# Scores and the product with V' as four column tiles of 32 rows in place of two of 64, in a cross-attention and feed-forward kernel

## The chip, the cores and the metric

One core of one Trainium2 chip. The metric is device microseconds of one execution. The engines are TensorE (PE in the profile, PEld for its weight loads), VectorE (DVE), ScalarE (ACT), GpSimd (POOL) and SyncE (SP), each with its own instruction stream; they meet through semaphores.

## What is computed

128 sequences of 64 tokens of 128 features (`x`) attend to 128 context sequences of the same shape, and a feed-forward part follows:

```python
def xattn(q, k, v, Wq, Wk, Wv, Wo, bo, mask):      # 16 heads of 64
    qh = split_heads(q @ Wq)
    kh = split_heads(k @ Wk)
    vh = split_heads(v @ Wv)
    dots = einsum('bhid,bhjd->bhij', qh, kh) * 64 ** -0.5
    dots = where(mask or causal, -max, dots)
    out = einsum('bhij,bhjd->bhid', softmax(dots), vh)
    return merge_heads(out) @ Wo + bo
x = x + xattn(layernorm(x), ctx, ctx, ...)
x = x + bitlinear(silu(bitlinear(layernorm(x), w_gate)) * bitlinear(layernorm(x), w_up), w_down)
```

`bitlinear` rounds its input to 8 bits by row and its weights to -1, 0, 1 times a scale.

## The kernel before, in words

The 8,192 tokens are taken as 64 pairs of sequences, 128 tokens each; four pairs are a group that is loaded with one DMA. The projections are folded: M = Wk Wq^T and N = Wv Wo are made once for each head in the setup, so that with K' = M ctx and V' = ctx N the scores of a head are x_norm K' and its output is prob V', both with 128 features in the middle or at the end. M, N and the context are each split in a high and a low part (`F32R`), and K' and V' are three matmuls each (`k_unit`, lines 323 to 325; `v_quarter`, lines 403 to 405).

Every engine runs the same list of slots, one a pair: eight written out, then a hardware loop over eight slots that is run six times (`slots`, whose loop is line 202), then eight written out and three of tail. In a slot TensorE does, in this order, which is written out by hand:

- the scores of pair s (line 432): for each half of the heads (8 heads x 64 keys are 512 columns, one bank of `ps_s`) and each of the two sequences b, one float32 matmul call whose stationary operand is that sequence's 64 columns of `xn_t` and whose output is 64 of the 128 partitions. Sequence b = 0 writes partitions 0 to 63 and b = 1 writes 64 to 127, so the two use different column tiles of the array. In the profile a float32 call is two weight loads and two matmuls.
- the transpose of the quantised rows of pair s - 1 (line 445, it waits for VectorE's `xq_b`, line 839), four of the hidden rows of pair s - 3 (line 453), the transposes of the probabilities of pair s - 1 (line 460), gate and up (lines 473, 474), the down product (line 489), among them the quarters of V' of pair s and of K' of the next group
- the product with V' of pair s - 1 (line 501): for each of 8 pairs of heads `a` and each sequence b one float32 call, stationary 64 columns of `prob_t`, moving 128 columns of `vp`, accumulated over `a` in `ps_a[b * S:(b + 1) * S, 0:D]`. It waits for `pt_evac`, `v_evac` and `x2_done` (the wait before it is line 498).
- two quarters of K' and V' more (the wait value of the last V' quarters is made at line 399), and after every fourth slot eight transposes of the next but one group (lines 281 and 317).

ScalarE evacuates K', V' and the transposes (line 521) and does the exponential (line 577). VectorE adds the bias to the scores (line 745, which signals `biased`), takes maxima and sums (lines 748, 821), adds the residual to the product with V' (line 808) and does the layer norms and the quantisation; once a group it makes the low part of the context (line 679). GpSimd subtracts the maxima and multiplies by the reciprocals (lines 875, 893). The setup's M products (line 310) have 64 rows: heads of one parity stand in rows 0 to 63 and write `ps_s`, those of the other stand in rows 64 to 127 and write `ps_kv`, in this order of the program, 16 matmuls each.

Of the kernel before, what the change touches and what calls it, by code (L numbers as in the profile page):

```python
# [32 lines left out]
P = 128  # L33
# [7 lines left out]
def build(nc, x, ctx, mask, wq, wk, wv, wo, bo, w_gate, w_up, w_down, ident, causal, chooser, out):  # L41
    B, S, D = x.shape
# [3 lines left out]
    HP = H // 2  # L46
# [7 lines left out]
    BANK = 512  # L54
# [6 lines left out]
    with ExitStack() as es:  # L61
# [5 lines left out]
        ps_s = ps("ps_s", 2)  # L67
        ps_kv = ps("ps_kv", 2)
        ps_a = ps("ps_a", 1)
# [29 lines left out]
        xn_t = [sb(f"xn_t{i}", [P, GP * P]) for i in range(2)]  # L99
# [5 lines left out]
        vp = [sb(f"vp{i}", [P, 2, HP, D]) for i in range(2)]  # L105
        prob = [sb(f"prob{i}", [P, H, S]) for i in range(2)]
        prob_t = sb("prob_t", [P, HP, P])
# [75 lines left out]
        def live(it, c, back=0):  # L183

            return not isinstance(it, int) or 0 <= BODY * it + c - back < PAIRS

        def group_ahead(it, c, n):

            return not isinstance(it, int) or 2 * it + c // GP + n < GROUPS

        def first(it, c):
            return isinstance(it, int) and it == 0 and c == 0
# [74 lines left out]
        def _(pe):  # L267
            mm = nc.tensor.matmul
# [5 lines left out]
            for k in range(8):  # L274
                mm(banks[k], choose[:], mask_bf[:, k * BANK:(k + 1) * BANK],
                   start=True, stop=True).then_inc(maskrow_ready, 1)
# [28 lines left out]
            for par in range(2):  # L305
                r = slice(DH * par, DH * par + DH)
                for half in range(2):
                    for k in range(4):
                        a = 4 * half + k
                        t = mm(banks[2 * par + half][:, k * P:(k + 1) * P], w_t[0][r, a, :], w_t[1][r, a, :],  # L310
                               start=True, stop=True)
# [72 lines left out]
            def slot(it, c):  # L384
                s = BODY * it + c
                g, q, par = 2 * it + c // GP, c % GP, c // GP % 2
# [31 lines left out]
                if live(it, c):  # L418

                    if q == 0:  # L420
                        pe.wait_ge(k_evac, 16 * g + 16)
                        pe.wait_ge(xnt_evac, g + 1)
                    if first(it, c):
                        pe.wait_ge(mean_done, 1)
                    if live(it, c, 1):
                        pe.wait_ge(v_evac, 8 * s - 2)
                        if not isinstance(it, int) or group_ahead(it, c - 1, 1):
                            pe.wait_ge(k_evac, 16 + 4 * s - 1)
                    for half in range(2):
                        for b in range(2):  # L430
                            cols = slice(q * P + b * S, q * P + b * S + S)
                            t = mm(ps_s[b * S:(b + 1) * S, half * BANK:(half + 1) * BANK], xn_t[par][:, cols],  # L432
                                   kp[par][:, half * 8:half * 8 + 8, cols], start=True, stop=True)
                    t.then_inc(scores_ready, 1)
                if first(it, c):
# [13 lines left out]
                if live(it, c, 3):  # L449

                    pe.wait_ge(hb_ready, s - 2)
                    for k in range(FB):
                        t = nc.tensor.transpose(ps_h[:, k * P:(k + 1) * P], hid_b[:, k * P:(k + 1) * P], id_bf[:])
# [29 lines left out]
                if live(it, c, 3):  # L483
# [4 lines left out]
                    for k in range(FB):  # L488
                        t = mm(ps_a[:, D:2 * D], hid_t[:, k, :], wd_t[:, k, :], start=(k == 0), stop=(k == FB - 1))
# [3 lines left out]
                if live(it, c, 1):  # L493

                    pe.wait_ge(pt_evac, 2 * s)
                    pe.wait_ge(v_evac, 8 * s)
                    if live(it, c, 3):
                        pe.wait_ge(x2_done, s - 2)
                    for a in range(HP):
                        for b in range(2):  # L500
                            t = mm(ps_a[b * S:(b + 1) * S, 0:D], prob_t[:, a, b * S:(b + 1) * S],  # L501
                                   vp[(c - 1) % 2][:, b, a, :], start=(a == 0), stop=(a == HP - 1))
                    t.then_inc(attn_ready, 1)
                v_quarter(2)
                k_quarter(2)
# [2 lines left out]
                if live(it, c) and q == GP - 1 and group_ahead(it, c, 2):  # L508
# [5 lines left out]
                    transpose_x(par)  # L514

            slots(pe, slot, 4 - 1)


# [405 lines left out]
```

## Time and profile before

| | |
|---|---|
| median of 3 runs | 829.24 us (828.57 to 829.48) |
| the profiled execution, first to last instruction (its span) | 827.9 us |
| mean granted TensorE clock of it | 0.991 |
| TensorE matmuls, busy | 781.9 us (94%) |
| VectorE, busy | 738.6 us (89%) |
| ScalarE, busy | 679.7 us (82%) |
| GpSimd, busy | 407.3 us (49%) |

The profile gives no time of that execution other than its span; the medians contain what lies around it. Matmuls overlap, and their ends are modelled by the profiler, so rates are taken from starts. In the rows L501 is line 501; `128*64 128x512` is 128 rows and 64 columns of stationary operand and a moving operand of 128 rows and 512 columns. Groups of the same kind that follow each other are merged, with their count behind an x; such a row's duration is from the first start to the last end, less idle time.

### The profile page before, as it was taken

How to read it: one execution, taken by the hardware profiler on the slowest of the kernel's cores; microseconds unless marked ns; L12 is line 12 of the kernel's file. 1: busy time of each engine (PE TensorE's matmuls, PEld its weight loads, DVE VectorE, ACT ScalarE, POOL GpSimd, SP SyncE). 2: the span in 40 equal slices, each digit the busy share in tenths (PEclk: the TensorE clock that was granted, in tenths of full speed). 3: DMA queues.
4: the chain of work that ended last, by engine and by line, in shares of the span. 5: the costliest groups of instructions: out<-in, count | busy, mean ns of one | idle time of the engine just before them, and what ended most of it. 6: DMA issues, size and time to landing. Idle time of an engine off the chain costs nothing.

```text
span 827.9 us, 17931 instructions
## 1 busy us (share of the span) xinstructions
PE 781.9 (94%) x5487; PEld 539.4 (65%) x5550; DVE 738.6 (89%) x1909; ACT 679.7 (82%) x1202; POOL 407.3 (49%) x404
## 2 busy tenths in 40 slices
PE   7899999999999999999999999999999999999873
PEld 5657666766766666676666667567666666766552
DVE  6759999999989998999989999899989999988994
ACT  4689888888888888888888898888888888888772
POOL 1235555454544644545455554455554555545551
PEclk9999999999999999999999999999999999999996
DMA  7200010100101010010100101010010100000000
GB/s 214 62 1 1 15 39 15 39 1 15 39 14 38 13 35 4 13 38 13 38 4 21 28 13 38 14 38 0 13 39 13 38 13 13 2 13 14 1 14 13
DMA packets 37108, 20.49 MB, mean 25 GB/s; under 512 B 1460, under 2 KB 36534, under 8 KB 37046
## 3 DMA queue, kind: packets, MB, share of 16 engines
q1 hardware_dynamic: 37046, 19.84, 8.3%
q14 instruction: 45, 0.37, 0.2%
q8 instruction: 17, 0.28, 0.1%
HBM read 15.64 MB, written 4.19 MB: 24 GB/s over the span
## 4 chain that ended last, share of the span: by engine, by line
PE 52%; DVE 31%; issue 11%; ACT 3%; DVEq 1%; POOL 1%; DMA 0%; POOLq 0%; ACTq 0%
PE ps_a L501 9%; PE ps_s L432 7%; DVE row_sum L821 5%; DVE xq_b L839 3%; PE ps_s L403 3%; DVE amax L778 2%; DVE hid L775 2%; PE ps_s L323 2%; PE ps_a L460 2%; PE ps_b L460 2%; PE ps_kv L403 2%; PE ps_s L325 2%; PE ps_kv L323 2%; PE ps_s L404 2%; PE ps_s L324 2%
## 5 line engine op out<-in xcount | busy, mean ns | idle before, releaser
L875 POOL TENSOR_TENSOR prob<-prob,row_max 128x1024 f32<-128x1024 f32 x64 | 122.0, 1906 | 194.1 <-DVE row_max L748 194.1
L521 ACT ACTIVATE vp<-ps_s 64x512 f32<-64x512 f32 x256 | 151.4, 591 | 32.8 <-PE ps_s L405 28.5
L893 POOL TENSOR_TENSOR prob<-prob,row_rec 128x512 f32<-128x512 f32 x128 | 130.9, 1044 | 56.2 <-DVE row_rec L823 56.2
L521 ACT ACTIVATE vp<-ps_kv 64x512 f32<-64x512 f32 x256 | 151.6, 592 | 5.4
L885 POOL TENSOR_TENSOR hid_b<-hid_q,neg_round 128x512 bf16<-128x512 f32 x64 | 66.6, 1041 | 130.1 <-DVE hid_q L792 130.1
L432 PE MATMUL ps_s<-kp,xn_t 128*64 128x512 f32 x512 | 124.0, 605 | 2.9 <-ACT vp L521 1.9
L501 PE MATMUL ps_a<-vp,prob_t 128*64 128x128 f32 x2048 | 125.9, 276 | 0.8 <-DVE x L770 0.6
L501 PEld LDWEIGHTS ps_a<-vp,prob_t 128*64 128x64 f32 x2048 | 110.6, 137 | 24.0 <-issue 16.4
L852 POOL TENSOR_TENSOR rs<-ve,neg_half 128x1 f32<-128x1 f32 x128 | 70.4, 550 | 35.5 <-DVE ve L670 25.4
L745 DVE TENSOR_TENSOR prob<-ps_s,bias_sb 128x1024 f32<-128x1024 f32 x64 | 78.2, 1222 | 10.7 <-PE ps_s L432 9.9
L521 ACT ACTIVATE kp<-ps_s 128x512 f32<-128x512 f32 x130 | 77.8, 598 | 12.0 <-PE ps_s L291 8.2
L748 DVE TENSOR_REDUCE row_max<-prob 128x16 f32<-128x1024 f32 x64 | 78.1, 1220 | 2.2
L821 DVE TENSOR_REDUCE row_sum<-prob 128x16 f32<-128x1024 f32 x64 | 77.4, 1210 | 0.0
L521 ACT ACTIVATE xq_t<-ps_u 128x128 bf16<-128x128 bf16 x64 | 17.8, 278 | 68.0 <-PE ps_u L445 68.0
L521 ACT ACTIVATE kp<-ps_kv 128x512 f32<-128x512 f32 x122 | 72.3, 592 | 0.6 <-PE ps_kv L291 0.5
L432 PEld LDWEIGHTS ps_s<-kp,xn_t 128*64 128x64 f32 x512 | 31.0, 136 | 60.5 <-issue 46.5
L577 ACT ACTIVATE prob<-prob 128x1024 f32<-128x1024 f32 x64 | 66.9, 1045 | 0.0
L839 DVE TENSOR_SCALAR xq_b<-xq 128x128 bf16<-128x128 f32 x64 | 61.2, 956 | 2.2
L403 PE MATMUL ps_s<-n_hi,ct_hi 128*128 128x512 f32 x128 | 62.4, 487 | 0.7 <-ACT vp L521 0.7
L403 PE MATMUL ps_kv<-n_hi,ct_hi 128*128 128x512 f32 x128 | 61.3, 479 | 0.0
L323 PE MATMUL ps_kv<-ct_hi,m_hi 128*128 128x512 f32 x120 | 52.6, 438 | 1.0 <-ACT wd_t L521 1.0
L323 PE MATMUL ps_s<-ct_hi,m_hi 128*128 128x512 f32 x128 | 52.1, 407 | 0.4
(176 smaller groups left out, 1767.6 us busy)
## 6 DMA issues: line engine op xcount, KB each, us to landing
x_in<-in_x SPq DMA_DIRECT2D x16, 256.0 KB, 3.0
ctx_in<-in_ctx SPq DMA_DIRECT2D x16, 256.0 KB, 3.4
x_res<-in_x SPq DMA_DIRECT2D x16, 256.0 KB, 2.8
out<-x SPq DMA_DIRECT2D x15, 256.0 KB, 2.3
kp<-in_L_xattn_Wk SPq DMA_DIRECT2D x1, 512.0 KB, 4.5
kp<-in_L_xattn_Wq SPq DMA_DIRECT2D x1, 512.0 KB, 5.3
kp<-in_L_xattn_Wv SPq DMA_DIRECT2D x1, 512.0 KB, 6.2
kp<-in_L_xattn_Wo SPq DMA_DIRECT2D x1, 512.0 KB, 6.1
```

Of the source, the lines that this page charges most:

```text
L323: mm(dst, hi, ct_hi[par][:], start=True, stop=False)
L403: mm(v_dst, ct_hi[par][:, cols], hi, start=True, stop=False)
L432: t = mm(ps_s[b * S:(b + 1) * S, half * BANK:(half + 1) * BANK], xn_t[par][:, cols], kp[par][:, half * 8:half * 8 + 8, cols], start=True, ...
L501: t = mm(ps_a[b * S:(b + 1) * S, 0:D], prob_t[:, a, b * S:(b + 1) * S], vp[(c - 1) % 2][:, b, a, :], start=(a == 0), stop=(a == HP - 1))
L521: copy = lambda dst, src, **kw: nc.scalar.activation(dst, src, ACT.Copy, **kw)
L745: v.tensor_tensor(prob[c % 2][:], ps_s[:, :].rearrange("p (h j) -> p h j", j=S), pair_bias.broadcast_to([P, H, S]), ALU.add).then_inc(bias ...
L748: v.tensor_reduce(row_max[c % 2][:], prob[c % 2][:], AX, ALU.max).then_inc(max_done, 1)
L821: v.tensor_reduce(row_sum[:], prob[c % 2][:], AX, ALU.add).then_inc(sum_step, 1)
L839: v.tensor_scalar(xq_b[:], xq[:], ROUND, None, ALU.subtract).then_inc(xq_ready, 1)
L852: p.tensor_tensor(dst[:], src[:], neg_half[:], ALU.pow).then_inc(done, 1)
L875: p.tensor_tensor(prob[c % 2][:], prob[c % 2][:], rows(row_max[c % 2]), ALU.subtract).then_inc(shifted, 1)
L893: p.tensor_tensor(prob[c % 2][:, heads, :], prob[c % 2][:, heads, :], rows(row_rec[c % 2])[:, heads, :], ALU.mult).then_inc(normed, 1)
```

## The change

Both calls are split by output rows: each writes 32 partitions instead of 64. The scores take 32 columns of `xn_t` with the same 512 moving columns of K' of their sequence, the product takes 32 columns of `prob_t` with the same 128 moving columns of V'. Order, semaphores, banks and results are as before.

```diff
                     for half in range(2):
-                        for b in range(2):
+                        for r in range(4):
+                            b = r // 2
+                            rows = slice(q * P + r * 32, q * P + r * 32 + 32)
                             cols = slice(q * P + b * S, q * P + b * S + S)
-                            t = mm(ps_s[b * S:(b + 1) * S, half * BANK:(half + 1) * BANK], xn_t[par][:, cols],
+                            t = mm(ps_s[r * 32:r * 32 + 32, half * BANK:(half + 1) * BANK], xn_t[par][:, rows],
                                    kp[par][:, half * 8:half * 8 + 8, cols], start=True, stop=True)
                     t.then_inc(scores_ready, 1)
...
                     for a in range(HP):
-                        for b in range(2):
-                            t = mm(ps_a[b * S:(b + 1) * S, 0:D], prob_t[:, a, b * S:(b + 1) * S],
-                                   vp[(c - 1) % 2][:, b, a, :], start=(a == 0), stop=(a == HP - 1))
+                        for r in range(4):
+                            rows = slice(r * 32, r * 32 + 32)
+                            t = mm(ps_a[rows, 0:D], prob_t[:, a, rows],
+                                   vp[(c - 1) % 2][:, r // 2, a, :], start=(a == 0), stop=(a == HP - 1))
                     t.then_inc(attn_ready, 1)
```

## Rows read from the trace of the kernel before

**Rows 1.** The page: busy time and share of each engine; the chain that ended last
```profile
PE 781.9 (94%) x5487; PEld 539.4 (65%) x5550; DVE 738.6 (89%) x1909; ACT 679.7 (82%) x1202; POOL 407.3 (49%) x404
...
PE 52%; DVE 31%; issue 11%; ACT 3%; DVEq 1%; POOL 1%; DMA 0%; POOLq 0%; ACTq 0%
PE ps_a L501 9%; PE ps_s L432 7%; DVE row_sum L821 5%; DVE xq_b L839 3%; PE ps_s L403 3%; DVE amax L778 2%; DVE hid L775 2%; PE ps_s L323 2%; PE ps_a L460 2%; PE ps_b L460 2%; PE ps_kv L403 2%; PE ps_s L325 2%; PE ps_kv L323 2%; PE ps_s L404 2%; PE ps_s L324 2%
```

**Rows 2.** Groups by line and shape: xcount | busy us, mean ns | idle before it
```profile
L501 PE MATMUL ps_a<-vp,prob_t 128*64 128x128 f32 x2048 | 125.9, 276 | 0.8 <-DVE x L770 0.6
L432 PE MATMUL ps_s<-kp,xn_t 128*64 128x512 f32 x512 | 124.0, 605 | 2.9 <-ACT vp L521 1.9 <-ACT kp L521 1.0
...
L501 PEld LDWEIGHTS ps_a<-vp,prob_t 128*64 128x64 f32 x2048 | 110.6, 137 | 24.0 <-issue 16.4 <-ACT prob_t L521 7.6
...
L404 PEld LDWEIGHTS ps_s<-n_lo,ct_hi 128*128 128x128 f32 x128 | 24.4, 190 | 0.1
```

**Rows 3.** Who waited for whom: us in total, times, longest us
```profile
PE ps_u L445 <- DVE xq_b L839: 14.6, 25, 3.9
...
DVE ct_lo L679 <- issue: 10.3, 5, 2.3
DVE prob L745 <- PE ps_s L432: 9.9, 12, 5.9
```

**Rows 4.** Chain of waits between 395 and 420 us: start us, us, what
```profile
404.77 1.90 PE ps_a L501 x32
...
409.67 1.87 PE ps_s L432 x8
```

**Rows 5.** Line 501, 404 to 407 us: xcount: min/median/max ns, first to last start
```profile
L501 PE MATMUL ps_a<-vp,prob_t x32: 272/273/323, 404.7 to 406.4; 128*64 128x128 f32 x32
```

**Rows 6.** Timeline of TensorE's matmuls, 14.8 to 16.7 us (setup, line 310)
```profile
16.31 0.37 PE L310 MATMUL ps_kv<-kp 64*128 64x128 f32 x1
16.42 0.27 PE L310 MATMUL ps_s<-kp 64*128 64x128 f32 x1
...
16.64 0.27 PE L310 MATMUL ps_s<-kp 64*128 64x128 f32 x1
```

**Rows 7.** Timeline of TensorE cut at 404.709 us: what had started by then
```profile
404.37 0.40 PE L325 MATMUL ps_s<-ct_hi,m_lo 128*128 128x512 f32 x1
404.70 0.33 PE L501 MATMUL ps_a<-vp,prob_t 128*64 128x128 f32 x2
```

**Rows 8.** Line 432, 409 to 412 us, columns as in rows 5
```profile
L432 PE MATMUL ps_s<-kp,xn_t x8: 592/592/643, 409.6 to 410.9; 128*64 128x512 f32 x8
```

**Rows 9.** Sequencer instructions of lines 498 and 399, 235.1 to 236.1 us
```profile
L498 PEldq EVENT_SEMAPHORE  x1: 51/51/51, 235.2 to 235.2; - x1
...
L399 PEldq ALU_OP  x1: 32/32/32, 236.0 to 236.0; - x1
```

**Rows 10.** One turn of the loop: us, then busy us (count) of PE, PEld, DVE, ACT, POOL
```profile
224.00:321.60 97.60, 94.91 (x673) 65.13 (x680) 89.61 (x234) 83.30 (x148) 50.62 (x51) 1.00 0.08 22
```

**Rows 11.** The loop's own instructions (line 202), 223 to 231 us, columns as in rows 5
```profile
L202 PEldq COMPARE_BRANCH  x1: 246/246/246, 224.0 to 224.0; - x1
L202 PEldq FUSED_REGOPS  x1: 59/59/59, 224.3 to 224.3; - x1
...
L202 DVEq COMPARE_BRANCH  x1: 63/63/63, 227.1 to 227.1; - x1
...
L202 DVEq FUSED_REGOPS  x1: 63/63/63, 230.3 to 230.3; - x1
```

**Rows 12.** Timeline of all engines, 226.5 to 231.2 us
```profile
226.92 1.94 PE L432 MATMUL ps_s<-kp,xn_t 128*64 128x512 f32 x8
...
230.99 1.22 DVE L745 TENSOR_TENSOR prob<-ps_s,bias_sb 128x1024 f32<-128x1024 f32 x1
```

**Rows 13.** DMA queues (packets, MB): 0 to 225 us; 225 to 719 us
```profile
q8 instruction: 12, 0.20, 0.4%
...
q14 instruction: 30, 0.25, 0.2%
```

## Prediction

> **What bounds the kernel now.** I read the page first: TensorE is busy 94% of the span and VectorE 89%, so two engines stand close to the bound, and the chain that ended last runs 52% over TensorE and 31% over VectorE [rows 1]. On it the product with V' (line 501) has 9% of the span and the scores (line 432) 7%. The groups by line then give the two edited steps: 512 and 2,048 matmuls, eight and 32 for each of the 64 pairs, 605 and 276 ns each [rows 2]. Last I read who waits. VectorE waited for the scores 9.9 us in 12 pairs, and TensorE for VectorE's quantised rows 14.6 us in 25 [rows 3]. So the lead changes hands inside every pair: what TensorE gains or loses in these two steps reaches the end only where it leads. The chain says where: 9% of 827.9 us is 74.5 us, about 39 pieces of the 1.90 us that one product takes on it, and 7% is 58 us, about 31 pieces of 1.87 us [rows 1, 4]. Of 128 groups some 70 count.
>
> **How many tiles run at once today.** A float32 product is two matmuls per call (1,024 calls, 2,048 records). One step's 32 matmuls last 273 ns each, and from the first start to the last are 1.7 us [rows 5]: over 31 steps 55 ns each. Float32 matmuls with the same 128 moving columns that share one tile start 0.11 us apart (the one at 16.42 and the one at 16.64 have one between them) [rows 6]. So two are in the array all the time, and two do start within 10 ns of each other [rows 7]. The scores are alike: eight matmuls of 592 ns, 1.3 us from first to last start [rows 8], which is three steps of 0.43 us (four times 0.11), not seven. Both tiles are full. What no stream hides is the first weights load: the first matmul of each tile shows 323 and 643 ns against 273 and 592 [rows 5, 8], so 51 ns.
>
> **The change, part by part.**
> 1. *Streams.* Calls double, 16 to 32 for the product with V' and 4 to 8 for the scores, each with as many moving columns as before, in four tiles for two. Per tile there are still 16 matmuls of 0.11 us and four of 0.43 us. Change: nothing, if four run at once as two do now.
> 2. *Weights loads.* 4,096 matmuls and 1,024 replace 2,048 and 512, each with a load of 32 columns for 64. Loads take 190 ns for 128 float32 columns and 137 for 64 [rows 2], 53 ns for 64 columns, so about 27 for 32. Exposed once per group: -26 ns. The others hide behind the stream of their own tile, as they do now.
> 3. *The last tile's lag.* The second tile follows the first by less than 10 ns [rows 7]; I take 7. The fourth follows by 21: +14 ns.
> 4. *Look-ahead.* Tiles can be fed together only if the engine passes over instructions that wait for a busy tile. In the setup, row tile two (into ps_kv) starts at 16.31 while row tile one (into ps_s) still has three matmuls to start, the last at 16.64 [rows 6]. So it passes waiting work, but it did so only with three matmuls (and two loads between them) left, and not earlier. For two column tiles that is ample: a call leaves one load and one matmul waiting. With four tiles three calls, six instructions, stand ahead of the fourth tile's first load. If the limit is five per tile nothing happens; if it is five in all, the fourth tile waits until a first load ends, 27 ns. Bounds: 0, and 60 ns if a further lag of that size builds up at later calls. I take 27, because the setup row is the only one that shows a limit.
> 5. *Issue.* The product step issues 128 instructions in 1.7 us for 64, 13.6 ns each. In the pair at 235 us the sequencer left the wait at line 498 at 235.2 and had the 64 instructions behind it handed over by 236.0, when it did line 399's register operation [rows 9]: at most 12.5 ns each. Enough, with 8% to spare. Cost 0; the cover is thin.
> 6. *The semaphores, the readers, the moments of switching between whole-array and column tiles* are as before: two switches for each group. What a switch costs with four tiles no row shows. Entering costs now 0.33 - 0.21 = 0.11 us (404.37 to 404.70 [rows 7]; the 0.21 is half a float32 stream of 512 columns, line 325 being of the single-pass kind). Bounds: -0.05 to +0.05 us; I take 0.
> 7. *Code.* The loop is eight pairs, 97.6 us, 673 matmuls and 680 loads [rows 10]; the change adds 40 and 40 a pair, 640 to 1,353, or 47%. See the second rival.
>
> Sum: -26 + 14 + 27 = +15 ns a group, times 70 is +1.05 us. Against the profiled span of 827.9 us that is 829.0; the median of the runs shown, 829.24, stands 1.37 us above the span, and carried over gives **830.3 us**. TensorE's work in all its 128 groups would rise by 1.9 us, and half stays hidden under VectorE. The measurement can tell 0.2% from no change, 1.7 us, so this is "no change".
>
> **Rivals.**
> *Only the lags count, upward (slower).* Five waiting instructions in all, and a tile falls behind at every second call: 60 ns instead of 27, and the 8% of issue cover gone in half the product steps (2 ns on each of 64 loads and matmuls, 128 ns). Then 70 groups x 48 ns (60 for 27 gives 48 for 15) + 20 x 128 ns = +5.9 us: 835. For it: the setup row. Against: the 12.5 ns is an upper bound. Chance 0.17.
>
> *Code is fetched anew at each turn of the loop (slower).* VectorE does this now: its branch is at 227.1 and its next sequencer instruction at 230.3 [rows 11], it stands idle before line 679 in 5 turns, 2.3 us at the longest and 10.3 in all [rows 3]. TensorE does not: branch at 224.0, next at 224.3 [rows 11], and queue 8 brings 12 packets up to 225 us and then none up to 719 us, where queue 14 fetches 30 [rows 13]. I read queue 8 as TensorE's; it can hold 1,353 matmuls and loads and their waits; whether it holds 1,993 no row shows. If not, TensorE resumes 3.1 us after its branch as VectorE does, or some 4 us, its packets being larger (0.20 MB / 12 against 0.25 / 30). It branches 2.9 us ahead of its next matmul (226.92 [rows 12]), so the scores come 0.3 to 1.3 us late. But VectorE takes them only at 230.99, though their last matmul ended at 228.86 [rows 12]: it is still held up by its own fetch, 2.1 us of cover. So I expect the fetch and price it at nothing. It decides from 5 us of stall on; exposed by 1 us in each of five turns it is +5 us: 835.5, and 838 with the lags. Chance 0.17.
> The Trainium skill (Runtime: NRT & Kernel Launch, Instruction fetch mechanics) gives TensorE room for 2,048 instructions and the others for 512, and says that a branch to a target outside forces a fetch. The trace agrees for VectorE; by that rule the longer loop, 1,993 and over a hundred waits and register operations, would not fit.
>
> *The matmuls start strictly in program order (much slower).* Each call's second matmul must then start, one stream after its first, before the next tile's first: four tiles are worth no more than two, and 32 calls of 0.11 us and eight of 0.43 make 3.5 us for 1.7 and 3.4 for 1.3, +3.8 us a pair, over 240 us in all: about 1,070. Against it: the ps_kv matmul that overtook three of ps_s [rows 6], and the two within 10 ns [rows 7]. Chance 0.03.
> The Trainium skill (TensorE: Matmul & The Clock Gate, Part 3) says just that, matmuls start in order and only loads are pulled ahead. The setup rows contradict it.
>
> *The change does less than it says, to the good (faster).* Without the look-ahead limit each group is 12 ns shorter: 70 x 12 = 0.8 us, 828.4, which still is "no change". To be seen, switching must get cheaper too: 50 ns at each end of a group is 70 x 0.11 = 8 us at most, 821; a third of that is 826. Nothing in the profile speaks for it but that fewer weights have to be loaded. Chance 0.08.
>
> *Forecast, 828.4 to 830.9:* chance 0.55.
>
> **How the numbers follow.** The likeliest value is 830.3. The range leaves out the in-order case and half of the faster one, and goes up to where fetch and lags come together: 827.0 to 838.0. Faster than by 0.2% is the last rival: 0.08. Within 0.2% is the forecast without its upper edge: 0.52. Slower takes both middle rivals, the in-order case and that edge: 0.17 + 0.17 + 0.03 + 0.03 = 0.40.
>
> **What would show it.** In the product step 64 matmuls, four starting within about 30 to 50 ns, and the group on the chain 1.87 to 1.97 us long for 1.90. In the scores 16 matmuls, 1.84 to 1.93 for 1.87. In both, the first matmuls shown as about 27 ns longer than the rest. VectorE's idle before line 745 and TensorE's before line 445 as now, within 2 us. Queue 8 with 70 to 80 packets, about ten a turn, a gap of 3 to 4 us between TensorE's branch and its next sequencer instruction, and the VectorE stall before line 679 as before. Wrong: a group above 2.0 us (the look-ahead or the issue rate is shorter than I read it), a VectorE start of line 745 later than scores plus 0.2 us after each turn (the fetch is exposed), or a gap at the switches that has changed.

## The result, and the profile after

Four column tiles are slower: a median of 833.08 us (4 runs, 832.18 to 833.40) against 828.90 for the kernel before on the same chip (4 runs, 828.25 to 829.48), a ratio of 1.005 with a 95% interval of 1.0038 to 1.0062. That is +4.2 us, where 830.3 was forecast and 1 us of cost. The profiled execution took 832.18 us, with a span of 830.4 us and a mean granted clock of 0.992 (0.991 before).

The page of the kernel after: engines, instruction queues, the chain, and the groups that answer to [rows 1, 2].

```profile
PE 780.4 (94%) x8046; PEld 530.6 (64%) x8110; DVE 739.1 (89%) x1909; ACT 678.2 (82%) x1202; POOL 406.9 (49%) x404
...
q8 instruction: 80, 1.31, 0.7%
q14 instruction: 45, 0.37, 0.1%
...
PE 64%; DVE 22%; issue 8%; ACT 4%; POOL 0%; DVEq 0%; DMA 0%; POOLq 0%; ACTq 0%
...
L434 PE MATMUL ps_s<-kp,xn_t 128*32 128x512 f32 x1024 | 126.0, 598 | 12.8 <-ACT vp L524 7.3
...
L504 PE MATMUL ps_a<-vp,prob_t 128*32 128x128 f32 x4096 | 125.5, 275 | 0.8 <-DVE x L773 0.6
L504 PEld LDWEIGHTS ps_a<-vp,prob_t 128*32 128x32 f32 x4096 | 108.4, 110 | 24.1 <-issue 16.4
```

Line 432 is now 434, 445 is 447, 501 is 504, 679 is 682 and 745 is 748. The matmuls have doubled at the same busy time: 276 and 605 ns each have become 275 and 598, with twice as many at once. A load of 32 columns takes 110 ns (137 for 64). "Issue" on the chain, time in which the engine waited for nothing that the profile shows, is 8% of the span for 11% before. Queue 8 brought 80 packets, where it had brought 17.

Then who waits, to be held beside [rows 3]:

```profile
DVE prob L748 <- PE ps_s L434: 15.4, 22, 5.9
PE ps_u L447 <- DVE xq_b L842: 14.6, 25, 3.7
...
DVE ct_lo L682 <- issue: 10.1, 5, 2.2
```

TensorE's wait for `xq_b` and VectorE's stall before `ct_lo` are unchanged. VectorE's wait for the scores is not: 15.4 us in 22 pairs for 9.9 in 12.

**The two steps themselves.** The instructions of line 504, then of line 434, in one pair in the middle of the run (the columns are duration ns min/median/max, then first and last start), as [rows 5, 8]:

```profile
L504 PEld LDWEIGHTS ps_a<-vp,prob_t x64: 106/110/110, 404.9 to 406.5; 128*32 128x32 f32 x64
L504 PE MATMUL ps_a<-vp,prob_t x64: 272/273/297, 404.9 to 406.6; 128*32 128x128 f32 x64
...
L434 PEld LDWEIGHTS ps_s<-kp,xn_t x16: 106/110/110, 409.8 to 410.7; 128*32 128x32 f32 x16
L434 PE MATMUL ps_s<-kp,xn_t x16: 592/592/617, 409.8 to 411.1; 128*32 128x512 f32 x16
```

And the timeline cut just after the product's start, as [rows 7]:

```profile
404.88 0.32 PE L504 MATMUL ps_a<-vp,prob_t 128*32 128x128 f32 x4
```

Four matmuls start within 25 ns, one in each tile: all four tiles are fed at once. By the single records, the 64 starts of the product now lie within 1,682 ns where the 32 lay within 1,695 (-13 ns); the scores' lie within 1,332 for 1,345 (-13 or -14 ns, by the pair). On the chain the product is one piece of 1.89 us for 1.90, the scores of 1.85 for 1.87:

```profile
404.95 1.89 PE ps_a L504 x64
...
409.86 1.85 PE ps_s L434 x16
```

So neither step has become longer, and the time must have gone elsewhere. The sequencer's share of line 202, the loop's own, shows where. These are its instructions at the first turn, and then the branch over all six passes (min/median/max). [Rows 11] had 246 ns for TensorE's branch.

```profile
L202 PEldq COMPARE_BRANCH  x1: 3658/3658/3658, 222.7 to 222.7; - x1
...
L202 DVEq COMPARE_BRANCH  x1: 63/63/63, 225.8 to 225.8; - x1
...
L202 PEldq FUSED_REGOPS  x1: 63/63/63, 226.4 to 226.4; - x1
L202 DVEq FUSED_REGOPS  x1: 63/63/63, 228.7 to 228.7; - x1
...
L202 PEldq COMPARE_BRANCH  x6: 82/3527/3679, 222.7 to 715.2; - x6
```

And this is what follows the branch on the timeline, TensorE's scores and VectorE's two steps, to be held beside [rows 12], where the eight matmuls stand in one piece and line 745 has no idle before it:

```profile
226.88 1.92 PE L434 MATMUL ps_s<-kp,xn_t 128*32 128x512 f32 x15 [1.21 <-ACT vp L524]
229.41 0.59 PE L434 MATMUL ps_s<-kp,xn_t 128*32 128x512 f32 x1 [0.62 <-issue]
...
228.79 0.69 DVE L682 TENSOR_TENSOR ct_lo<-ps_b,ct_hi 128x512 fp32r<-128x512 f32 x1 [1.99 <-issue]
230.15 1.22 DVE L748 TENSOR_TENSOR prob<-ps_s,bias_sb 128x1024 f32<-128x1024 f32 x1 [0.67 <-PE ps_s L434]
```

There are **two stalls on TensorE**. The first ends with the branch: the scores start 1,481 ns after the matmul before them started, where it was 202, so they are 1.28 us late. The second stands inside the scores. Fifteen matmuls have started by 228.20; the sixteenth, the one that signals VectorE, starts only at 229.41, though its load of weights had started at 227.78. The first stall is covered: VectorE's own code stall ends at 228.79 with `ct_lo`. The second is not: VectorE waits 0.67 us for the last matmul before line 748. In the five turns that wait is 0.67, 0.70, 1.26, 0.57 and 0.60 us, 3.8 us together, and in the pair after it a further 0.3 us each. The sixteenth matmul itself starts 1.2 to 1.8 us after the fifteenth. The granted clock is 1.00 in all five stretches, so a slower clock is no part of it. At the third turn:

```profile
425.54 0.69 DVE L682 TENSOR_TENSOR ct_lo<-ps_b,ct_hi 128x512 fp32r<-128x512 f32 x1 [1.97 <-issue]
427.49 1.23 DVE L748 TENSOR_TENSOR prob<-ps_s,bias_sb 128x1024 f32<-128x1024 f32 x1 [1.26 <-PE ps_s L434]
```

One turn of the loop by the table of windows, and the instruction queues between the first turn and the end of the loop (packets, MB), as [rows 10, 13]:

```profile
222.70:321.20 98.50, 95.47 (x994) 64.42 (x1002) 90.01 (x236) 83.25 (x149) 50.86 (x51) 1.00 0.08 24
...
q8 instruction: 54, 0.88, 0.7%
q14 instruction: 30, 0.25, 0.2%
```

From TensorE's first branch to its last (222.7 to 715.2) are 492.5 us, where it was 487.9 (224.0 to 711.9): 0.9 us more in each of five turns, 4.6 us in all. Pair by pair, the time from one pair's product to the next differs by at most 0.12 us between the traces, mostly by under 0.03, in the straight-line slots before the last and in the six later slots of each turn. The shift grows in the two pairs after each of the five turns alone: by 0.63, 0.93, 1.51, 0.89 and 0.93 us, 4.9 us. In those same turns queue 8 fetches, 54 packets where before it fetched none. The two profiled spans differ by only 2.5 us (830.4 and 827.9): in the trace after, the first product starts 1.2 us earlier, the last pair is 0.6 us shorter, and the small differences make up the rest. The medians, 4.2 us apart, are what the change costs.

So the theory to be tested: the four tiles cost nothing; with the 640 added instructions TensorE's loop no longer stays in the engine from turn to turn, it is fetched anew at each turn, and what is paid for is the second stall of each turn, since it falls on the scores. The rivals: (A) the scores' tiles themselves, their signal 21 ns later (below); (B) a small cost in every group; (C) the fetches as such, as traffic or issue; (D) the first stall.

### The profile page after: what moved, and what is told of

It is laid out like the page before. It is cut to its first block, busy times and chain, and to the rows that moved or that the text cites. A ratio compares the mean times of both kernels' runs of the same rounds, so it can differ in the third digit from the quotient of the medians.

```text
span 830.4 us, 23050 instructions
## 1 busy us (share of the span) xinstructions
PE 780.4 (94%) x8046; PEld 530.6 (64%) x8110; DVE 739.1 (89%) x1909; ACT 678.2 (82%) x1202; POOL 406.9 (49%) x404
## 3 DMA queue, kind: packets, MB, share of 16 engines
q8 instruction: 80, 1.31, 0.7%
## 4 chain that ended last, share of the span: by engine, by line
PE 64%; DVE 22%; issue 8%; ACT 4%; POOL 0%; DVEq 0%; DMA 0%; POOLq 0%; ACTq 0%
PE ps_a L504 10%; PE ps_s L434 10%; PE ps_s L403 4%; DVE row_sum L824 3%; DVE xq_b L842 3%; PE ps_s L323 3%; PE ps_b L462 3%; PE ps_kv L403 3%; PE ps_a L462 3%; PE ps_s L404 2%; PE ps_s L405 2%; PE ps_kv L323 2%; PE ps_s L325 2%; PE ps_kv L324 2%; PE ps_s L324 2%
## 5 line engine op out<-in xcount | busy, mean ns | idle before, releaser
L434 PE MATMUL ps_s<-kp,xn_t 128*32 128x512 f32 x1024 | 126.0, 598 | 12.8 <-ACT vp L524 7.3
L504 PE MATMUL ps_a<-vp,prob_t 128*32 128x128 f32 x4096 | 125.5, 275 | 0.8 <-DVE x L773 0.6
L504 PEld LDWEIGHTS ps_a<-vp,prob_t 128*32 128x32 f32 x4096 | 108.4, 110 | 24.1 <-issue 16.4
L748 DVE TENSOR_TENSOR prob<-ps_s,bias_sb 128x1024 f32<-128x1024 f32 x64 | 78.3, 1223 | 16.2 <-PE ps_s L434 15.4
L434 PEld LDWEIGHTS ps_s<-kp,xn_t 128*32 128x32 f32 x1024 | 26.8, 109 | 67.8 <-issue 53.9
```

Of the source, the lines that this page charges most:

```text
L434: t = mm(ps_s[r * 32:r * 32 + 32, half * BANK:(half + 1) * BANK], xn_t[par][:, rows], kp[par][:, half * 8:half * 8 + 8, cols], start=True, ...
L504: t = mm(ps_a[rows, 0:D], prob_t[:, a, rows], vp[(c - 1) % 2][:, r // 2, a, :], start=(a == 0), stop=(a == HP - 1))
L748: v.tensor_tensor(prob[c % 2][:], ps_s[:, :].rearrange("p (h j) -> p h j", j=S), pair_bias.broadcast_to([P, H, S]), ALU.add).then_inc(bias ...
```

## The experiments

All runs stand beside runs of the kernel before on the same chip, whose medians were 828.66 to 829.25 us.

**Scores alone** (e1_scores4). The first half of the change, the product left at two tiles:

```diff
-                        for b in range(2):
+                        for r in range(4):
+                            b = r // 2
+                            rows = slice(q * P + r * 32, q * P + r * 32 + 32)
...
-                            t = mm(ps_s[b * S:(b + 1) * S, half * BANK:(half + 1) * BANK], xn_t[par][:, cols],
+                            t = mm(ps_s[r * 32:r * 32 + 32, half * BANK:(half + 1) * BANK], xn_t[par][:, rows],
```

> Only the scores run as four tiles; the product with V' stays as before. TensorE's loop grows by 128 loads and matmuls to 1,481 for 1,353. Theory A (the loss is the code that TensorE fetches anew at each turn of the loop, and four tiles cost nothing by themselves): no fetch in the loop, queue 8 brings no packet between about 230 and 710 us, TensorE's branch takes 0.1 to 0.25 us as before, the time is that of the kernel before, 829 us, within 0.5 us. Theory B (the four tiles cost by themselves, through the scores that are signalled some 20 ns later after their last matmul starts and the 40 more loads and matmuls of a pair): the scores carry a part of the +4 us, 1 us or more, spread evenly over the pairs.

Measured: 828.85 us (827.95 to 829.36, 11 runs) against 829.01, ratio 0.9998 (0.9989 to 1.0007). TensorE's branch and VectorE's wait for the scores:

```profile
L202 PEldq COMPARE_BRANCH  x6: 76/210/242, 222.9 to 710.2; - x6
...
DVE prob L747 <- PE ps_s L434: 10.1, 12, 5.9
```

Queue 8 has 19 packets in the whole run. The scores' four tiles cost nothing, and a loop that is only 128 instructions longer isn't fetched again. (A) is out.

**Product alone** (e2_product4). The other half, scores left at two tiles:

```diff
-                        for b in range(2):
-                            t = mm(ps_a[b * S:(b + 1) * S, 0:D], prob_t[:, a, b * S:(b + 1) * S],
-                                   vp[(c - 1) % 2][:, b, a, :], start=(a == 0), stop=(a == HP - 1))
+                        for r in range(4):
+                            rows = slice(r * 32, r * 32 + 32)
+                            t = mm(ps_a[rows, 0:D], prob_t[:, a, rows],
+                                   vp[(c - 1) % 2][:, r // 2, a, :], start=(a == 0), stop=(a == HP - 1))
```

> Only the product with V' runs as four tiles; the scores stay as before. The loop has 1,865 loads and matmuls and some 140 waits and register operations. Theory A: the code is fetched anew at each turn (queue 8 with 60 to 80 packets, a branch of 3.5 us), and the loss is most of that of the change, +2 to +5 us, all of it in the first two pairs after each turn; how much depends on where the first block of code ends. Theory B: each pair gains 13 ns in the product, so the time is 828 to 829 us or, if instructions cost by their number, +3 us spread evenly over all pairs.

Measured: 833.47 us (830.36 to 836.90, 6 runs), ratio 1.0055 (1.0034 to 1.0075), with 71 packets on queue 8. Its turns are not alike. At the second, TensorE's branch, the scores, and VectorE's step:

```profile
L202 PEldq COMPARE_BRANCH  x1: 4734/4734/4734, 320.4 to 320.4; - x1
...
325.64 3.37 PE L432 MATMUL ps_s<-kp,xn_t 128*64 128x512 f32 x8 [2.38 <-ACT xn_t L522]
...
329.17 1.23 DVE L746 TENSOR_TENSOR prob<-ps_s,bias_sb 128x1024 f32<-128x1024 f32 x1 [2.14 <-PE ps_s L432]
```

The scores, still two tiles of 64, take 3.37 us instead of 1.94. This is not the second stall. TensorE's sequencer had handed the scores over and was at line 448, behind them, by 326.02, so no code was missing; what fell was the granted clock, which the table of windows has in the column behind POOL's, after the counts:

```profile
325.60:326.00 0.40, 0.35 (x2) 0.20 (x4) 0.00 (x0) 0.00 (x0) 0.00 (x0) 1.00 0.16 41
326.00:329.40 3.40, 3.40 (x9) 0.96 (x6) 0.93 (x2) 0.00 (x0) 0.00 (x0) 0.50 0.01 2
...
329.50:331.00 1.50, 1.45 (x13) 1.00 (x12) 1.47 (x2) 0.77 (x3) 0.00 (x0) 1.00 0.00 0
```

TensorE had stood idle for 2.38 us behind the branch of 4.7 us, started the scores at 325.64, and from 326.01 to 329.42 ran at 0.50, the lower of its two levels (1.2 GHz for 2.4): a load took 226 to 231 ns for 133 to 136, a matmul up to 1,061 for 592. That turn alone, from branch to branch, is 2.5 us longer than before (99.94 for 97.46). In the other four turns the scores are whole at 1.00, VectorE waits for nothing before line 746, and a turn costs 0.0 to 0.2 us more than before.

So a refetch can perhaps cost in a second way: a longer first stall, and then a lower clock on the work behind it. The profiled execution shows the two once, one behind the other; that the first brought the second about is not shown. The median's +4.5 us is not explained by it: the other five executions have no trace, only granted clocks of 0.985 to 0.990 over the whole, where the kernel before beside them had 0.988 to 0.993.

**The change with TensorE's slots written out** (e3_after_pe_straight). The tiles stay, the turns go:

```diff
+        def slots(eng, slot, tail, straight=False):
...
+            if straight:
+                for it in range(BODIES):
+                    for c in range(BODY + tail * (it == BODIES - 1)):
+                        slot(it, c)
+                return
...
-            slots(pe, slot, 4 - 1)
+            slots(pe, slot, 4 - 1, straight=True)
```

> The changed kernel with TensorE's slots all written out (no loop, so no branch, for TensorE alone; the other engines keep theirs). Arithmetic, order and waits are those of the changed kernel. Theory A: the loss of 4 us goes, 828 to 829.5 us; VectorE's idle time before the low part of the context stays at 10 us in 5 turns. Theory B: it stays at 832 to 833 us.

Measured: 828.62 us (827.12 to 830.21, 12 runs), ratio 0.9995 (0.9986 to 1.0003). The page's instruction queues:

```profile
q8 instruction: 65, 1.06, 0.6%
q14 instruction: 45, 0.37, 0.1%
```

The tiles cost nothing that could be told over 64 pairs, so (B) is out. So is (C): 65 packets are still fetched, ahead of their use along a straight line, and they cost nothing.

**The change, its code moved by 40 instructions** (e4_after_shift). Waits on a semaphore that has long been set stand ahead of the slots on TensorE, so that the same loop lies elsewhere in the blocks in which code is fetched. The compiler makes 40 instructions of the 80 lines.

```diff
+            for _ in range(80):
+                pe.wait_ge(const_set, 1)
             pe.wait_ge(mask_step, 2)
```

> The changed kernel with 40 more semaphore waits at TensorE's start, while it waits for the mask anyway, so that its loop begins 40 instructions later in its block of code and the next block begins behind the scores of the first pair and not between their last two matmuls. Theory A in its finer form (each turn has two stalls, one at the branch that VectorE's own fetch hides, and one in the middle of the scores that nothing hides): the branch still takes 3.5 us, queue 8 still has about 80 packets, but the scores after a turn take 1.33 us from first to last start again and most of the loss goes, 829 to 830.5 us. If the stall at the branch alone is what counts, 832 to 833 us.

Measured: 828.58 us (827.84 to 829.49, 11 runs), ratio 0.9993 (0.9984 to 1.0002), a little below the lower end of what was expected: the whole loss is gone, not most of it. Queue 8 has 75 packets. TensorE's branch over all passes, and the first turn:

```profile
L202 PEldq COMPARE_BRANCH  x6: 83/3502/3788, 223.8 to 711.7; - x6
...
227.66 1.92 PE L436 MATMUL ps_s<-kp,xn_t 128*32 128x512 f32 x16 [0.93 <-ACT vp L526]
...
230.16 0.69 DVE L684 TENSOR_TENSOR ct_lo<-ps_b,ct_hi 128x512 fp32r<-128x512 f32 x1 [2.29 <-issue]
230.77 1.22 DVE L750 TENSOR_TENSOR prob<-ps_s,bias_sb 128x1024 f32<-128x1024 f32 x1
```

This is the run that decides for the change as a whole. The refetch is there (75 packets, 3.5 us at each branch), the first stall is there (0.93 us idle before the scores), all four tiles are there; but the sixteen scores matmuls stand in one piece, and line 750 starts when VectorE is free. (D) is out too, as long as VectorE's stall covers it: what cost 4.2 us was the place of the second stall.

**Product as four tiles in odd slots only** (e5_product4_odd). A loop of 1,753 instructions, counting the sequencer's, in the compiled program:

```diff
+                        if c % 2:
+                            for r in range(4):
...
+                            continue
                         for b in range(2):
```

> The product with V' runs as four tiles in the odd slots of the eight only, the scores as two. The loop has 1,609 loads and matmuls. It asks where the room for code ends: 1,481 (the scores alone) were not fetched anew, 1,865 (the product alone) were. If the room is simply 2,048 instructions, the loop fits and the time is 829 us. If whole blocks of the packets' size count, with one more fetched ahead, the loop, which by its place in the code touches eight blocks, does not fit: some ten packets of queue 8 a turn, a branch of 3.5 us, 829 to 833 us depending on where the first block ends.

Measured: 828.79 us (827.67 to 829.95, 10 runs) against 829.25, ratio 0.9994 (0.9985 to 1.0003). The branch over all passes, and the first turn:

```profile
L202 PEldq COMPARE_BRANCH  x6: 83/3582/3744, 223.9 to 711.6; - x6
...
227.85 1.94 PE L432 MATMUL ps_s<-kp,xn_t 128*64 128x512 f32 x8 [1.03 <-ACT vp L527]
...
230.60 1.22 DVE L751 TENSOR_TENSOR prob<-ps_s,bias_sb 128x1024 f32<-128x1024 f32 x1
```

Fetched anew at each turn (65 packets in all, 44 of them in the loop), and again hidden, since no second stall stands in the scores. Of five lengths of the loop in this case, 1,497 (before) and 1,625 (scores alone) stay resident; 1,753, 2,009 (product alone) and 2,137 (after) do not. These are lengths in the compiled program; the traces have one record less a turn, with a matmul for each load.

**Before, with VectorE's slots written out** (e6_before_dve_straight). This takes away the cover: VectorE's own stall of 2 us at each turn.

```diff
-            slots(dve, slot, 3)
+            slots(dve, slot, 3, straight=True)
```

> The kernel before with VectorE's slots written out, TensorE's and the other engines' in their loop. It takes VectorE's branch away, and with it its idle time before the low part of the context (2.0 to 2.3 us in 5 turns). In the kernel before, the first two pairs after a turn take about 1.5 us longer than at the loop's entry; if that is VectorE's fetch, this is 5 x 1.5 = 7 us faster than before, 821 to 823 us. If something else holds those pairs, under 2 us.

Measured: 820.54 us (819.71 to 823.01, 5 runs), ratio 0.9902 (0.9885 to 0.9918): 8.7 us faster than the kernel before by the medians, 8.1 by the ratio, where 7 was expected. VectorE's idle before `ct_lo` is now of another kind and small:

```profile
DVE ct_lo L684 <- ACT ct_hi L526: 1.2, 8, 0.2
```

**The moved code of e4 with VectorE's slots written out** (e7_shift_dve_straight). TensorE's fetch as in e4, and no cover over it. The edits are those of e4 and e6.

> The changed kernel with the 40 waits at its start (whose second stall is gone) and VectorE's slots written out, so that TensorE's stall at the branch stands alone. Theory A (VectorE's own fetch hid it): it comes 1.3 us late in each of five turns with nothing to cover it, so this is 4 to 7 us slower than the kernel before with VectorE written out, about 827 to 829 us, and no more than 1 us from the kernel before. If the branch costs nothing by itself, 821 to 823 us.

Measured: 825.91 us (825.80 to 826.77, 5 runs), ratio 0.9961 (0.9947 to 0.9974). It is 5.4 us above e6, inside the 4 to 7 expected. The time itself missed: 827 to 829 and at most 1 us from the kernel before were expected, and it is 3.3 us below that kernel. In part that is because e6 had come out below its own 821 to 823; and 5.4 us do not use up the 8.7 that e6 had gained. The first turn:

```profile
227.34 1.92 PE L441 MATMUL ps_s<-kp,xn_t 128*32 128x512 f32 x16 [1.35 <-ACT vp L531]
...
227.26 0.69 DVE L689 TENSOR_TENSOR ct_lo<-ps_b,ct_hi 128x512 fp32r<-128x512 f32 x1
229.32 1.23 DVE L755 TENSOR_TENSOR prob<-ps_s,bias_sb 128x1024 f32<-128x1024 f32 x1 [1.37 <-PE ps_s L441]
```

VectorE is ready for its step at 227.95 (227.26 + 0.69) and waits 1.37 us for the scores. The same first stall that cost nothing in e4 now costs 1.1 us at each turn (5.4 / 5): VectorE's stall was the cover of TensorE's.

**All engines' slots written out**, with four tiles in both steps (e8_after_all_straight), with two (e9_before_all_straight), and with four in the product alone (e10_product4_all_straight). On top of the kernel in question:

```diff
-            slots(pe, slot, 4 - 1)
+            slots(pe, slot, 4 - 1, straight=True)
...
-            slots(act, slot, 3)
+            slots(act, slot, 3, straight=True)
...
-            slots(dve, slot, 3)
+            slots(dve, slot, 3, straight=True)
...
-            slots(pool, slot, 3)
+            slots(pool, slot, 3, straight=True)
```

> The changed kernel with the slots of all four computing engines written out. No engine but SyncE branches. Four tiles cost nothing by themselves, so this should be as fast as the kernel before with VectorE written out, 821 to 823 us, or a little faster, since no engine's fetch is left: 820 to 823 us.

> The kernel before (two tiles) with the slots of all four computing engines written out: the partner of the changed kernel in that form (820.1 us), so that four tiles and two are compared where neither fetches anew. If four tiles cost and gain nothing, 820 to 820.5 us. By the trace of the changed kernel a pair gains 13 ns in the product and loses 7 in the scores, which is 0.4 us at most over 64 pairs. If each load or matmul more costs something by itself, this is 1 us faster or more: 819 us or less.

> The product with V' as four tiles, the scores as two, all slots written out. If the product's 13 ns and the scores' earlier signal both reach the end, 0.5 to 1.3 us faster than the form with both as four tiles: 819 to 819.6 us. More likely they are lost under VectorE, and it is within 0.5 us of 820.1 us.

Measured: 820.14 us (819.43 to 820.19), 819.96 (819.93 to 821.68) and 820.34 (820.11 to 821.67), four runs each; ratios to the kernel before 0.9887, 0.9902 and 0.9899, each with an interval of about 0.0015 to 0.0017 either way. With no loop on any engine, two tiles and four differ by 0.2 us, less than can be told. All three beat both kernels of this case by some 9 and 13 us, and e6 alone brings nearly the same: what the loops cost was VectorE's refetch.

## Why the prediction came out as it did

The median, 833.08, lies inside the range of 827.0 to 838.0, but not where the likeliest case stood (828.4 to 830.9), and slower, which had 0.40, not "no change", is what happened. By its own steps:

1. **Streams** (nothing): right. Four run at once as two did, with the same busy time.
2. **Loads** (-26 ns) and 3. **the last tile's lag** (+14 ns), together -12: -13 and -14 were measured between first and last start. The price of a load was the estimate that the rows gave: the first matmul stands 24 ns over the others, as forecast (27), for 50.
4. **Look-ahead** (+27 ns): the term that was mis-sized; it is 0. There is no limit of five here: the four tiles' first matmuls start at 404.883, .890, .896 and .903, and the fourth tile's first load with them, past six instructions of the first three calls that had not started. The setup row on which I rested the term has another cause, which nothing here shows.
5. **Issue** (0): right. At the first turn 92 of the step's 128 instructions had started when the sequencer did line 399's register operation 1,139 ns after the group's start, so 36 were handed over and waiting: the engine was not starved. 6. **Switching** (0): the next matmul after the product starts 202 ns after its last one, as before.
7. Sum: +15 ns a group was forecast. The product got 13 ns shorter. The scores lost 21 ns again that no step had: VectorE's step starts 775 ns after the start of the last of them, where it was 754, so that they come out at +7. The runs with no refetch at the turns (e1, e3) and with no loops (e8 against e9) give no difference for all of it that could be told: -0.2, -0.4 and +0.2 us.

**The lag rival** (835) fell with term 4, as did the case of strict program order: four starts within 25 ns. The Trainium skill (TensorE: Matmul & The Clock Gate, Part 3) has matmuls start in the order of the program; this trace is against it, since the first call's own second matmul starts 133 ns after its first, behind the first ones of the three other tiles, and no run came near the 1,070 us of strict order.

**The fetch rival** was the mechanism, and every sign that it named appeared: 80 packets, ten or eleven in a turn, a branch of 3.5 us for 0.2, the scores 1.28 us late at the first turn, and that lateness hidden under VectorE's own stall, which e4 and e5 show with the cover and e7 without it. One sign of the forecast failed, and gave the loss away: VectorE's idle before line 745, "as now, within 2 us", rose by 5.5 us. The step that failed is its price, "price it at nothing". I followed the branch to its target and stopped there. Of what a refetch costs, that is only the first block; the code after it has to arrive as well, and the next block begins at the last matmul of the scores, the one that VectorE waits for, as the gap in the trace and the move by 40 instructions in e4 show. The cover of 2.1 us ends with the first stall and has nothing left for a second. "It decides from 5 us of stall on" was wrong in the same way: the branch never took more than 3.7 us, and the turn still lost 0.9. The exposed case was given "1 us in each of five turns", 835.5, for want of a row. Its size a turn was right (0.9), by luck: it priced the first stall left uncovered, and what was paid was the second. Its time was 2.4 us too high: 830.3 contained +1.05 of tiles that cost nothing, the kernel before had 828.90 beside this run for 829.24, five turns cost 4.2 for 5, and 830.3 and 5 are 835.3. The upper end of the range, 838, was said to be fetch and lags together; by the text's own terms these are 5 and 5.9 us on 829.24, about 840. 833.08 lies inside the range with either.

On the room: the Trainium skill (Runtime: NRT & Kernel Launch, Instruction fetch mechanics) gives TensorE 2,048 instructions, by which the loop after does not fit, and it doesn't. But the 1,753 of e5 don't fit either, so that figure is no safe limit for a loop. The prediction said that the trace agrees for VectorE. It does on the branch that fetches, but not on the room of 512: VectorE's loop has 450 records a turn, under 512, and is fetched anew at each turn, six packets of queue 14.

All five lengths agree with a count in whole blocks. A packet of queue 8 is 16.4 KB (1.31 MB / 80), and where TensorE's slots are written out (e3, e8, e9, e10) there are 256.3 to 256.5 records, a matmul for each load, to a packet. Take blocks of 256, and let one begin at the last matmul of the scores after the branch, where the kernel after stalls. Counted on from there, the loops lie in 7 blocks (before), 7 (scores alone), 8 (e5), 9 (product alone) and 10 (after); the first two stay, and the others bring 8.8, 9.4 and 10.8 packets a turn (e4, with 9 blocks, 9.8). So what fits is what lies in at most seven such blocks, perhaps with one more read ahead. That is a fit to five kernels, not a measurement of the memory. By the same count e2's first block ends some 160 instructions behind the branch's target, far behind its scores, which is one more sign that its slow scores were no stall for code.

What stays open: why the second stall in the kernel after is 1.2 us at one turn and 1.8 at another; why e2's branch once took 4.7 us and those of the kernel after never more than 3.7; and with it, what the unprofiled executions of e2 lost, why they spread over 6.5 us, and whether it was the clock each time.

## What to carry to other kernels

Before an edit adds instructions to a hardware loop, count that engine's instructions in a turn, with its register and branch instructions, and look in the profile whether its instruction queue is silent between the turns; the step from silent to fetching is worth more than most edits in the loop. Once it fetches, look past the branch: find which instruction begins the next block, who waits for it, and whose stall hides it; forty idle instructions ahead of the loop took away a loss of 4.2 us here. And before a slow stretch behind a stall is called a second stall, look at the granted clock and at where the sequencer is: in e2 the code was there and the clock was at half. Two column tiles in place of one share the array, but cutting each in half again, with the same moving columns per call, gives nothing where both tiles were full.

## What was not expected of the hardware

- Read in a straight line, code costs nothing: e3 fetches 65 packets of 16.4 KB at 828.62 us. Stalls came only behind a branch to code that was no longer there: at the branch (3.5 us on TensorE in the median, 4.7 at most) and, in the kernel after, at the next block. Writing out VectorE's loop, with 12 packets of queue 14 between 225 and 719 us for 30, took 8.1 to 8.7 us off.
- The end of the scores is seen 21 ns later with tiles of 32 columns (775 ns from the last matmul's start to VectorE's step, for 754). No run shows why.
- Matmuls of a free column tile overtake those that wait for a busy one from the first call of a step on: the fourth tile starts 20 ns after the first, with six predecessors not started.
- Behind the longest stall for code the clock was lower as well, in the one execution that shows it: in e2, after a branch of 4.7 us and 2.38 us without a matmul, the granted clock fell to 0.50 for 3.4 us, 0.37 us after TensorE had begun again.
